# Index copies, rank picks and GpSimd's wait moved by a block in the spline passes of a four-layer graph network

## The reference

```python
h0 = x @ w[0]
h1 = x @ w[1]
msg = (1.0 - uc) * h0[src] + uc * h1[src]
agg = segment_sum(msg, dst) / max(deg, 1)
return agg + x @ root + bias
```

## Time and profile before

| | us |
|---|---|
| median of three runs (lowest, highest) | 20,927.28 (20,924.93, 20,939.71) |
| span of the profiled execution | 21,015.3 |
| first spline pass, window | 2,565 |
| second spline pass, window | 2,567 |
| GpSimd busy over the span | 12,061.3 (57%) |
| VectorE busy | 8,986.5 (43%) |
| TensorE busy | 8,764.9 (42%) |

### The profile page before, as it was taken

How to read it: one execution, slowest core, us unless ns; L and a number is a source line. 1 busy time by engine, 2 the same in 40 slices (tenths; PEclk the granted TensorE clock), 3 DMA queues, 4 the chain that set the end, 5 groups by cost and what they waited for, 6 DMA issues and landing times. The chain is left out here.

```text
span 21015.3 us, 206080 instructions
## 1 busy us (share of the span) xinstructions
PE 8764.9 (42%) x55813; PEld 7722.6 (37%) x55813; DVE 8986.5 (43%) x25576; ACT 2713.0 (13%) x7595; POOL 12061.3 (57%) x11797
## 2 busy tenths in 40 slices
PE   3444444444323222232244554455545545454543
PEld 2333333333223233232212444344433334454553
DVE  3444433333334344443497444444434444233333
ACT  1222212222100000000032111111111111000000
POOL 4666656666566666666601566666656666455554
PEclk9999999999999999999965666666666666555555
DMA  1222212222222222222274000000000000111111
GB/s 56 61 61 61 61 59 80 81 82 81 65 78 82 82 79 81 82 81 82 85 261 162 11 11 11 11 11 11 11 12 22 22 21 22 27 44 44 44 43 37
DMA packets 575621, 1217.97 MB, mean 58 GB/s; under 512 B 229172, under 2 KB 326681, under 8 KB 547750
## 3 DMA queue, kind: packets, MB, share of 16 engines
q0 software_dynamic: 378560, 478.90, 10.6%
q1 hardware_dynamic: 182900, 679.92, 8.9%
q10 hardware_dynamic: 14112, 58.61, 0.8%
HBM read 560.22 MB, written 656.36 MB: 58 GB/s over the span
## 5 line engine op out<-in xcount | busy, mean ns | idle before, releaser
L795 POOL DMA_INDIRECT rows<-gcn_table,index x3430 | 3735.1, 1089 | 2508.8 <-ACT index L803 1513.2
L516 POOL DMA_INDIRECT rows<-spline_table,index x3136 | 3232.8, 1031 | 2103.8 <-ACT index L534 1140.2
L850 PE MATMUL p_slots<-part,lo_t 128*128 128x208 bf16 x18816 | 2690.6, 309 | 2890.1 <-ACT lo_t L812 1349.7
L850 PEld LDWEIGHTS p_slots<-part,lo_t 128*128 128x128 bf16 x18816 | 2079.9, 119 | 3373.5 <-issue 2762.5
L1036 POOL DMA_INDIRECT sent<-a_msg,a_place x1568 | 1575.3, 1005 | 1213.5 <-DVE a_run L1151 739.8
L1371 POOL DMA_INDIRECT e_rows<-soft_table,e_index x1568 | 1509.9, 963 | 1237.1 <-ACT e_index L1379 757.6
L1092 PE MATMUL a_p_label<-tw,a_label 8*128 8x64 f32 x3136 | 1000.0, 400 | 2030.6 <-issue 1647.3
L868 DVE TENSOR_TENSOR one_lo<-iota,lo 128x2560 bf16<-128x2560 f32 (+1 forms) x297 | 733.4, 2469 | 2587.3 <-ACT index L803 2339.5
L1028 POOL DMA_INDIRECT a_rows<-att_table,a_index x1568 | 1506.3, 961 | 484.6 <-issue 474.1
L1092 PEld LDWEIGHTS a_p_label<-tw,a_label 8*128 8x128 f32 x3136 | 854.1, 318 | 1999.4 <-issue 1917.1
L812 ACT ACTIVATE lo_t<-p_turn 128x512 bf16<-128x512 bf16 x1287 | 717.9, 595 | 5133.9 <-remote 3326.4
(11 more groups left out here) (394 smaller groups left out, 17452.9 us busy)
## 6 DMA issues: line engine op xcount, KB each, us to landing
running_dst<-a_run SPq DMA_DIRECT2D x98, 1600.0 KB
running_src<-s_run SPq DMA_DIRECT2D x98, 1600.0 KB
s_rows<-sent ACTq DMA_DIRECT2D x98, 584.0 KB
rows<-gcn_table,index POOLq DMA_INDIRECT x3430
running<-e_run SPq DMA_DIRECT2D x98, 528.0 KB
running<-run SPq DMA_DIRECT2D x98, 520.0 KB
rows<-spline_table,index POOLq DMA_INDIRECT x3136
running<-run SPq DMA_DIRECT2D x98, 512.0 KB
```

Of the source, the lines that this page charges most:

```text
L516: pool.indirect_dma_start(out=rows[h][:, k, :], out_offset=None, in_=table, in_offset=offsets(index[h][:, k:k + 1])).then_inc(gathered[h], 16)
L795: pool.indirect_dma_start(out=rows[h][:, ON_CHIP + k, :], out_offset=None, in_=table, in_offset=offsets(index[h][:, k:k + 1])).then_inc(ga ...
L850: ins = nc.tensor.matmul(p_slots[:, m, 0:CLASS * SLICE], lo_t[h][:, k, q, :], flat(part[:, c, q * CLASS:(q + 1) * CLASS, :]), start=q == 0 ...
```

## The change

Four things are done in `spline_pass`. Index blocks are copied two blocks ahead: two before the loop, and in the loop the copy of block n+2 into `index[h]`, after the gathers of block n have arrived. GpSimd waits itself for the step at which VectorE has used up the rows (MADE = 2 steps into the block two before). `p_look` has two halves, and the pick and the reduction of block n-1 are done in VectorE's block n, in front of the one-hots; the first block has a memset in their place, and the last pick comes behind the loop. The padding of `src_i` grows by a block, and the first of VectorE's rounds is written out so that it can be told apart.

```diff
-            p_look = ctx.enter_context(nc.psum_tensor(f"p_look{uid}", [P, RANKED, C], F32))
+            p_look = ctx.enter_context(nc.psum_tensor(f"p_look{uid}", [P, 2, RANKED, C], F32))
-        INIT = per
+        INIT = 2 * per
+        MADE = 2
...
                     pool.wait_ge(indexed[h], i + 1)
+
+                    pool.wait_ge(stepped, INIT + per * (2 * i + h - 2) + MADE)
...
             stage_index(0, 0)
+            stage_index(1, B)
             stage(0, 0)
             with act.Fori(0, IT) as i:
                 for h in range(2):
                     n = 2 * i + h
 
-                    act.wait_ge(stepped, INIT + per * n - (per - 2))
-                    stage_index(1 - h, (n + 1) * B)
+                    act.wait_ge(gathered[h], 16 * B * (i + 1))
+                    stage_index(h, (n + 2) * B)
...
-                            nc.tensor.matmul(p_look[:, kk, 0:J], lo_tf[q % 2][:, k, :], seen[q % 2][:], start=True, stop=False)
+                            nc.tensor.matmul(p_look[:, h, kk, 0:J], lo_tf[q % 2][:, k, :], seen[q % 2][:], start=True, stop=False)
...
+            def pick(h, half, step):
+                dve.wait_ge(looked, Q * half)
+                step(nc.vector.tensor_tensor(picked[:], p_look[:, h, :, 0:J], one_hi[h][:], ALU.mult))
+
+            def rank_of(at, step):
+                step(nc.vector.tensor_reduce(edge["rank"][:, at], picked[:], AX.X, ALU.add))
...
+                    skipped = rank and first and h == 0
+                    if rank and not skipped:
+
+                        pick(1 - h, half, step)
+                        after()
+                        rank_of(bass.ds((half - 1) * B + ranked, RANKED), step)
...
                     if count or rank:
                         one_hots(1 - h, step)
-                    if rank:
-
-                        dve.wait_ge(looked, Q * (2 * i + h + 1))
-                        step(nc.vector.tensor_tensor(picked[:], p_look[:, :, 0:J], one_hi[h][:], ALU.mult))
-                        after()
-                        step(nc.vector.tensor_reduce(edge["rank"][:, bass.ds((2 * i + h) * B + ranked, RANKED)], picked[:], AX.X, ALU.add))
+                    if skipped:
+                        step(nc.vector.memset(picked[:], 0.0), 2)
                     assert n[0] == per
...
+            both_halves(0, True)
+            with dve.Fori(1, IT) as i:
+                both_halves(i, False)
+            if rank:
+                done = lambda ins, by=1: ins.then_inc(stepped, by)
+                dve.wait_ge(stepped, INIT + per * 2 * IT)
+                pick(1, 2 * IT, done)
+                dve.wait_ge(stepped, INIT + per * 2 * IT + 1)
+                rank_of(slice((2 * IT - 1) * B + ranked, (2 * IT - 1) * B + B // 2 + ranked), done)
...
-        src_i = sb("src_i", [P, T + B], I32)
+        src_i = sb("src_i", [P, T + 2 * B], I32)
```

More of the change, by code:

```diff
@@ L620, in ranks @@
                             kk = q * GROUP + k
-                            nc.tensor.matmul(p_look[:, kk, 0:J], lo_tf[q % 2][:, k, :], seen[q % 2][:], start=True, stop=False)
+                            nc.tensor.matmul(p_look[:, h, kk, 0:J], lo_tf[q % 2][:, k, :], seen[q % 2][:], start=True, stop=False)
                             for j in range(k + 1):
-                                ins = nc.tensor.matmul(p_look[:, kk, 0:J], earlier[q % 2][:, PAIR[j] + k - j, :], one_hi[h][:, q * GROUP + j, :], start=False, stop=j == k)
+                                ins = nc.tensor.matmul(p_look[:, h, kk, 0:J], earlier[q % 2][:, PAIR[j] + k - j, :], one_hi[h][:, q * GROUP + j, :], start=False, stop=j == k)
                         ins.then_inc(looked, 1)
@@ L655, in _, with both_halves, step @@
                 one_hots(0, lambda ins: ins.then_inc(stepped, 1))
-            with dve.Fori(0, IT) as i:
+            def pick(h, half, step):
[3 more added lines that the diff above has]
+                step(nc.vector.tensor_reduce(edge["rank"][:, at], picked[:], AX.X, ALU.add))
+            def both_halves(i, first):
                 for h in range(2):
                     n = [0]
-                    def step(ins):
-                        ins.then_inc(stepped, 1)
-                        n[0] += 1
+                    def step(ins, by=1):
+                        ins.then_inc(stepped, by)
+                        n[0] += by
                     def after():
                         dve.wait_ge(stepped, INIT + per * (2 * i + h) + n[0])
+                    half = 2 * i + h
                     dve.wait_ge(staged[h], i + 1)
@@ L673, in _ @@
                     step(nc.vector.tensor_tensor(msg[h][:, :, 0:C], msg[h][:, :, 0:C], rows[h][:, :, 0:C], ALU.add))
+                    assert n[0] == MADE
                     dve.wait_ge(stored[h], 16 * (1 + len(cleared)) * i + 16)
@@ L683, in _ @@
                     if count:
-                        dve.wait_ge(counted, 1 + B * (2 * i + h))
+                        dve.wait_ge(counted, 1 + B * half)
                     if count or rank:
                         one_hots(1 - h, step)
-                    if rank:
-                        dve.wait_ge(looked, Q * (2 * i + h + 1))
-                        step(nc.vector.tensor_tensor(picked[:], p_look[:, :, 0:J], one_hi[h][:], ALU.mult))
-                        after()
-                        step(nc.vector.tensor_reduce(edge["rank"][:, bass.ds((2 * i + h) * B + ranked, RANKED)], picked[:], AX.X, ALU.add))
-                    assert n[0] == per
-            dve.wait_ge(stepped, INIT + per * 2 * IT)
+                    if skipped:
+                        step(nc.vector.memset(picked[:], 0.0), 2)
+                    assert n[0] == per
+            both_halves(0, True)
[7 more added lines that the diff above has]
+                rank_of(slice((2 * IT - 1) * B + ranked, (2 * IT - 1) * B + B // 2 + ranked), done)
+            dve.wait_ge(stepped, INIT + per * 2 * IT + 2 * rank)
             nc.vector.tensor_copy(final[:, 0:width], run[1][:, B - 1, :]).then_inc(stepped, 1)
@@ L1726, in _ @@
                     step(V.memset(w_labels[:], 0.0))
-                    for t in (src_i, keep, ew_s, rank, u_s, dst_lo, dst_hi, src_lo, src_hi):
+                    step(V.memset(src_i[:, T:T + 2 * B], 0))
+                    for t in (keep, ew_s, rank, u_s, dst_lo, dst_hi, src_lo, src_hi):
                         step(V.memset(t[:, T:T + B], 0))
```

## The result

The changed kernel takes 21,135.36 us (median of four runs, 21,121.12 to 21,163.79), the kernel before 20,926.1 us beside it. The ratio is 1.0104, with a 95% interval of 1.009 to 1.0119: slower by 1%.

A forecast was written before the change was run, and what follows sets the result against it. It took the spline passes to be bound by waits, TensorE's signals coming late while GpSimd issues gathers. Terms +20 - 29 + 25 = +16 us on 20,927 gave near 20,940 us; the 8-in-10 range was 20,620 to 21,290.

The forecast's parts named there:

- A: Both spline passes: bursts of gathers hold back the ring, the period stays; 20,850 to 21,010 us, chance 0.40.
- the sum of +16 us: Whole kernel: +20 us for GpSimd's own wait, -29 for pairs, +25 at pass ends, giving near 20,940 us.
- rival C: Spline passes: more bursts run back to back and starve the ring; 21,260 us if half the blocks do; chance 0.29.
- What bounds the kernel: Spline passes: no engine is full; waits bind, as TensorE's signals come late while GpSimd issues gathers; 26.0 us a block.
- the ring: TensorE's and ScalarE's rank chain in each spline block, 14.0 us by itself, 12.6 after the pick moves.
- Ordinary block of the second pass: A block ending with signals 2.7 us after the last issue; claimed to stay at 25.4 us despite the shorter ring.
- D: Spline passes: the 1.4 us cut from the ring counts in every block, 274 us faster, 20,653 us; chance 0.22.
- GpSimd's own wait: Wait for VectorE's two products before a burst: no stall, 0.1 us for the instruction, +20 us over 196 blocks.
- The end of a pass: Behind the last burst two blocks of ranks are left instead of one: 12.6 us, twice, +25 us.
- Pairs: Two blocks whose end the ring sets, not the burst; 21 counted (14 and 7), each 1.4 us shorter: -29 us.
- wherever they stand, so the burst keeps its length: First pass: VectorE's one-hots slide to the burst's first 8 us; GpSimd issues slower under them, 1.072 against 0.990 us.
- Rival B: Spline passes: GpSimd becomes the bound, its idle time vanishes; 912 us faster, 20,015 us; chance 0.09.

The follow-up runs named there:

- the repetition: Changed kernel, unedited, run again beside the kernel before on another chip: 21,295.03 us against 21,015.84, ratio 1.0144.
- the lead alone: Changed kernel with pick and reduction put back behind their own block's one-hots: 17,292.6 us (ratio 1.0) with signals in time, 21,283.71 us (1.0146) with signals late.

## Why the prediction was right in its range, and wrong in its likeliest case

21,135 us lies in the stated range, but the likeliest case, A (20,850 to 21,010), did not happen as a whole, and the sum of +16 us stands against +209. The chances did not choose a sign either: faster had 0.38, slower 0.37. That the range holds is owed to rival C, which set its upper end; for the sum, which leads to 20,940, it is luck.

- **What bounds the kernel.** Late signals of TensorE while GpSimd issues: right for the first measurement and three chips. A rest of 3.3 us inside the burst lets the ring through, and the stretch from stage to the second `seen` takes 10.2 us on the chip where nothing is late, 21.7 us in the kernel before. It is no property of the program alone: on that one chip the kernel before takes 17% less time.
- **Ordinary block of the second pass.** A: the block stays at 25.4 us, ended by `earlier` about 2.7 us after the last issue. Measured 25.16 and 2.6. D is refuted there, since cutting 1.4 us from the ring moved the block by 0.2.
- **GpSimd's own wait, 0.1 us a block.** Measured 0.10 us in blocks with a pause. That it costs no stall depends on the moved pick: without it, it was the last to end in 82 blocks of the second pass.
- **The end of a pass, +25 us.** From the last issue's end to the last pick's start it went from 19.5 to 27.3 us and from 20.5 to 31.3: +19 us.
- **Pairs, -29 us: the step that failed.** The term counted 21 pairs, as many as before, each 1.4 us shorter. In the second pass pairs and all else came to -16.8 us in the first measurement, and to +37 us in the repetition. In the first pass there are 38 long gaps instead of 5, and it grew by 173.5 us. Rival C had this mechanism and its price, 58.8 us for two blocks against 57.3 in the pair shown, and a rough sum gives the size: 33 more pairs x (57.3 - 2 x 26.0) = 175 us. (It is rough because 26.0 already holds the old pairs.) C set it at 6.8 us a pair for half of the blocks of both passes; it was 5.3 us a pair for 66 of the 196 blocks, all in the first pass.
- **Why C decided.** The prediction said of the one-hots that they slow the issues "wherever they stand, so the burst keeps its length". The length is indeed the same, 21.87 against 21.98 us. But their place matters for the ring: `at_lo` starts 10.3 us into the burst before, and 4.3 us into the burst behind the pause shown after. Cutting the destination one-hots took the first pass from 38 long gaps to 14. The likely way is that the slowed issues (2.33 and 1.72 us above) now fall where the ring is still running, and it comes through before the burst ends; this is argued from the rows. That the place of the one-hots could matter was named as a possible error, but stood in the sum at nothing. They are not all of it: the lead alone, with the one-hots in their old order, makes 22 long gaps.
- **Rival B.** It gave 20,015 us. On the chip with signals in time its picture of the passes holds in every block: 97 x (26.0 - 22.2 + 26.0 - 20.8) = 873 us less with the lead alone than in the earlier trace rows, where B had 912. But the change is not what brings it, since the kernel before takes the same time there. The Trainium skill's rule ("SBUF — State Buffer", SBUF: two separate sides), that TensorE and ScalarE never wait on anyone, is said of SBUF's ports. The trace of that chip agrees with it; with signals late, ScalarE waits 32.77 us for TensorE in the row above, and no run here shows whether a port has a part in that.

Left open: what makes a chip show the late signals; why a slowed issue or a rest lets TensorE's signals through; and why every seventh burst, that is one in 112 gathers, is 2 to 3 us longer, on the chip with signals in time too (23.9 against 21.5 us in the lead alone). SP's store, which slid with the one-hots, was not tried by itself. The changed kernel as it is was not run on the chip with signals in time; only its parts were.

## What to carry to other kernels

Before giving a producer more lead, ask what its pause was good for: here the pause between bursts was when the slower ring got its signals, and with the pick moved and more lead the first pass lost it in 55 of 97 gaps. When a loop of several engines runs far above its own length, measure that length bare and try a short rest inside the producer's burst; 3.3 us of rest turned a loss of 1% into a gain of 1% against the kernel before. A moved instruction has a place as well as a cost: sum it once for the engine that runs it and once for who runs beside it.

## What was unexpected of the hardware

The same unchanged kernel took 17,289 us on one chip and 20,979 to 21,030 us on three others. In the traces of the first TensorE's signals are in time while GpSimd issues, in those of the others they are late. Most of the difference lies behind the spline passes: 12,790 us against 15,567 behind the last gather of the lead-alone kernel. A gain or loss of 1% may thus hold in one condition only.

TensorE's granted clock fell to 0.65 in the second pass after (1.00 before), and from 5,700 to 10,371 us, in the attention pass, it was 0.50, its 1.2 GHz level, where the kernel before had 1.00, 2.4 GHz, from 5,545 to 10,216. GpSimd issued 3,040 gathers and scatters in that stretch of 4,671 us after and 3,030 before: the clock cost nothing here.

While VectorE's long compare `at_lo` runs, an issue of GpSimd takes up to 2.33 us instead of 0.94, and the burst of the first pass is 0.6 to 0.8 us shorter when the destination one-hots are cut to one step (21.03 us against 21.64 and 21.87 in the two traces of the changed kernel).
